# Two more sum banks for the last stage, later edge walks, last stores behind a load, and zero products in the pauses of a four-layer graph kernel

## The reference

```python
agg = segment_sum(h[src], dst) / max(deg, 1)      # SAGE, twice: relu(conv 1), then conv 2
out = agg @ W_l + b + h @ W_r
out = segment_sum((h @ W)[src] * edge_weight, dst) + b            # GCN
agg = segment_sum(concat(h[src], edge_attr) @ W_message, dst)     # message
z = layernorm(relu(agg) + h); z = z + mlp(z) (3 layers with skips); out = layernorm(h + z)
out = h @ W_self + segment_sum(top32(h @ W_neigh)[src], dst) / max(deg, 1)   # MaxK
```

## Time and profile before

| | |
|---|---|
| median of the runs | 1699.55 us |
| the profiled execution | 1700.06 us, span 1698.3 us |
| TensorE busy | 93% of the span |
| VectorE, ScalarE, GpSimd busy | 57%, 37%, 19% |
| DMA | 145 GB/s in the mean |

### The profile page before, as it was taken

The page is one execution under the profiler, slowest core; times in us unless marked ns, Lnnn a source line. Parts: engine busy times, 40 slices in busy tenths (PEclk is TensorE's granted clock), DMA queues, the critical chain, the costliest instruction groups (busy, mean ns, idle before and its releaser), DMA issues.

```text
span 1698.3 us, 41805 instructions
## 1 busy us (share of the span) xinstructions
PE 1580.5 (93%) x11011; PEld 1223.6 (72%) x11012; DVE 960.0 (57%) x2841; ACT 627.2 (37%) x1718; POOL 330.3 (19%) x926
## 2 busy tenths in 40 slices
PE   2899999999979999899997999999999999996996
PEld 1555565555657777678886888888878888874885
DVE  5788888878842122232335666666636777774111
ACT  6677787877731111111112222222224444440000
POOL 1565675656620000000000000000012111120000
PEclk8999999999999999999999999999999999997998
DMA  4266575757596766433354655666432221211444
GB/s 133 70 171 180 145 207 146 199 147 205 146 270 198 204 193 193 136 114 118 133 161 124 168 160 160 169 174 177 120 111 71 80 80 62 79 60 69 146 153 153
DMA packets 353541, 245.57 MB, mean 145 GB/s; under 512 B 195242, under 2 KB 337382, under 8 KB 353510
## 3 DMA queue, kind: packets, MB, share of 16 engines
q1 hardware_dynamic: 353510, 245.19, 50.4%
HBM read 138.17 MB, written 99.31 MB: 140 GB/s over the span
## 4 chain that ended last, share of the span: by engine, by line
issue 60%; PE 32%; DVE 3%; POOL 2%; DVEq 1%; SPq 0%; DMA 0%; POOLq 0%
PE ps L1386 21%; PE ps L1475 8%; POOL work L651 2%; PE ps L1429 1%; PE ps L1427 1%; DVE e_buf L1005 1%; DVE work L951 0%; PE ps L1421 0%; DMA arena<-turned_blocks 0%; SPq L419 0%; PE ps L1362 0%; DVE small L1262 0%; PE ps L1374 0%; DVE e_buf L1021 0%; PE ps L1379 0%
## 5 line engine op out<-in xcount | busy, mean ns | idle before, releaser
L1475 PE MATMUL ps<-arena 128*128 128x256 f16 (+1 forms) x5000 | 610.5, 274 | 21.8 <-DMA arena<-cnt_blocks 8.2
L1475 PEld LDWEIGHTS ps<-arena 128*128 128x128 f16 x5000 | 488.4, 98 | 122.9 <-issue 53.5
L1386 PE MATMUL ps<-e_buf 128*128 128x400 bf16 (+1 forms) x2476 | 376.6, 308 | 23.6 <-DVE e_buf L1005 23.5
L1386 PEld LDWEIGHTS ps<-e_buf 128*128 128x128 bf16 x2476 | 219.1, 98 | 169.9 <-DVE e_buf L1005 53.9
L1469 PE MATMUL ps<-arena 128*128 128x256 f32 x1250 | 278.5, 379 | 1.3 <-DMA arena<-wgt_blocks 1.3
L1469 PEld LDWEIGHTS ps<-arena 128*128 128x128 f32 x1250 | 235.4, 190 | 32.4 <-issue 1.5
L636 POOL TENSOR_SCALAR e_buf<-e_buf,w_col 128x128 bf16<-128x128 bf16 x600 | 225.0, 390 | 159.4 <-DVE e_buf L1001 152.1
L651 POOL TENSOR_TENSOR work<-work 128x256 f32<-128x256 f32 x75 | 54.5, 727 | 995.9 <-ACT work L844 995.9
L1005 DVE TENSOR_SCALAR e_buf<-iota,off_g,front 128x400 bf16<-128x400 f16 (+1 forms) x619 | 220.2, 402 | 32.9 <-issue 21.3
L1001 DVE TENSOR_SCALAR e_buf<-iota,front 128x128 bf16<-128x128 f16 x419 | 114.7, 279 | 44.4 <-PE ps L1386 30.0
L677 ACT ACTIVATE e_buf<-e_buf,front 128x128 bf16<-128x128 bf16 x219 | 88.3, 403 | 106.7 <-DVE e_buf L1001 104.9
(11 more groups left out here) (214 smaller groups left out, 1571.4 us busy)
## 6 DMA issues: line engine op xcount, KB each, us to landing
arena<-turned_blocks SPq DMA_DIRECT2D x75, 800.0 KB, 4.3
wgt_blocks<-arena SPq DMA_DIRECT2D x25, 1600.0 KB, 10.3
arena<-wgt_blocks SPq DMA_DIRECT2D x25, 1600.0 KB, 8.3
cnt_blocks<-work SPq DMA_DIRECT2D x25, 800.0 KB, 5.5
turned_blocks<-arena SPq DMA_DIRECT2D x25, 800.0 KB, 3.6
e_raw<-edge_features_padded SPq DMA_DIRECT2D x25, 576.0 KB, 7.8
edge_features_padded<-in_edge_attr SPq DMA_DIRECT2D x24, 512.0 KB, 9.9
out<-arena SPq DMA_DIRECT2D x24, 128.0 KB
```

Source lines behind the costliest of these rows:

```text
L1386: return pe.matmul(bank[:, 0:wide], rows_, cols, start=start, stop=True, skip_group_check=True)
L1475: m = pe.matmul(agg[par][:, 0:wide], BLK16[par][:, b * P:(b + 1) * P], ZH[zin(i)][:, b * ZW + part * D:b * ZW + part * D + wide], start=(b ...
```

## The change

Four things change. TensorE runs products of a zero tile with itself into bank 7 in four pauses of the preparation. The last chunk's counts are still stored ahead of load(2), but its weights behind it, and its edge features behind the third turn of late weights; ScalarE's wait for that weights store moves to the first z. In `row_layer`, walk 0 moves behind the first blocks of tile 1 and walk 1 behind tile 1, and `early` behind tile 1. In the last stage tiles 2 and 3 have sum banks 7 and 5 and blocks in the unused upper halves of the buffers, and are begun early too; the tiles from 4 on run as before. The diff, cut:

```diff
@@ sync
-            def store(c, par):
-                pad_edges(c)
+            def store_counts(c, par):
                 wait(sp, s_taken, c * PER + (PER + CR))
                 sp.dma_start(cnt_dram[...], ...).then_inc(s_store_c[par], 16)
+            def store_weights(c, par):
                 sp.dma_start(wgt_dram[...], ...).then_inc(s_store_w[par], 16)
...
-            store(NT - 1, 0)
+            store_counts(NT - 1, 0)
...
                     load(2, 2, 1, 0)
+                    store_weights(NT - 1, 0)
                     load(3, 3, 1, 1)
...
                     for turn in range(3):
                         keep_and_load(2 + turn, turn)
+                    pad_edges(NT - 1)
...
+                elif i == 4:
+                    for n in range(2):
+                        load(n, NT * i + n, None, n)
+                    for n in range(2):
+                        sp.dma_start(BLKX[n], turned_dram[2 + n]).then_inc(s_blkx[n], 16)
+                    tiles(sp, i, load, first=4)
@@ scalar, sage1
                     copy_transpose(g - 2, par)
+                    act.wait_ge(s_store_w[0], 16 * (NPAIR + 1))
                     first_z(n - 2, g - 2, par, ZH[1], conv_scale)
                 if isinstance(n, int) and n == 1:
                     act.wait_ge(s_scale, SCALE_CONV)
-                    for par_ in range(2):
-                        act.wait_ge(s_store_w[par_], 16 * ((NT + 1 - par_) // 2))
+                    act.wait_ge(s_store_w[1], 16 * NPAIR)
@@ vector, last
-                chain(dve.scalar_tensor_tensor(out=urow, in0=agg[1 - par][:, 0:D], scalar=one(rdeg, n),
+                from_ = agg_x[n - 2] if isinstance(n, int) and n in (2, 3) else agg[1 - par]
+                chain(dve.scalar_tensor_tensor(out=urow, in0=from_[:, 0:D], scalar=one(rdeg, n),
...
-            tiles(dve, PH_MAXK, last)
+            for n in range(4):
+                last(n, NT * PH_MAXK + n, None, (NT * PH_MAXK + n) % 2)
+            tiles(dve, PH_MAXK, last, first=4)
@@ tensor, preparation
+            def keep_running(rounds):
+                with pe.Fori(0, rounds):
+                    for k in range(8):
+                        pe.matmul(ps[:, 7, 0:P], zeros[:, :], zeros[:, :], start=True, stop=True,
+                                  skip_group_check=True)
             pe.wait_ge(s_const, 10)
+            keep_running(18)
             pe.wait_ge(s_prep, PREP_ROWS)
...
+            keep_running(14)
             pe.wait_ge(s_prep, PREP_SCAN)
...
+            keep_running(16)
             pe.wait_ge(s_prep, PREP_STEPS - 3)
...
+            keep_running(7)
             pe.wait_ge(s_prep, PREP_STEPS)
@@ tensor, aggregate
-            def aggregate(i, n, q, h, par, b0, b1):
-                if b0 == 0:
-                    wait(pe, s_blk[par], h * 16 + 16)
+            def aggregate(i, n, q, h, par, b0, b1, further=False):
+                into, counts = (agg_x[par], BLKX[par]) if further else (agg[par], BLK16[par])
+                if b0 == 0 and further:
+                    wait(pe, s_blkx[par], 16)
+                elif b0 == 0:
+                    wait(pe, s_blk[par], h * 16 + (0 if i == 4 and not (isinstance(n, int) and n < 2) else 16))
                     wait(pe, s_aggfree, q - 1 + CR)
@@ tensor, row_layer
-                if beside:
-                    beside(0)
                 z_ready(i)
                 aggregate(i, 0, q0, q0 // 2, q0 % 2, NT - 1, NT)
-                if early:
-                    early()
                 def body(n, q, h, par):
                     ...
                     aggregate(i, n, q, h, par, 0, c0)
                     if beside:
-                        beside(n)
+                        beside(0 if isinstance(n, int) and n == 1 else n)
                     transpose_rows(q + (NT - 1), par)
                     ...
-                tiles(pe, i, body, first=1, peel=1 if late_step else 0)
+                body(1, q0 + 1, (q0 + 1) // 2, (q0 + 1) % 2)
+                if early:
+                    early()
+                if beside:
+                    beside(1)
+                tiles(pe, i, body, first=2)
@@ tensor, inter and the last stage
-                    elif n < NT + 2 and b0 < final:
-                        begun_early(4, b0, min(b1, final), n - NT)
+                    elif n < NT + 4 and n != NT + 2 and b0 < final:
+                        begun_early(4, b0, min(b1, final), n - NT if n < NT + 2 else 2)
...
+            begun_early(4, final_early, NT - 2, 2)
+            begun_early(4, 0, NT - 2, 3)
             z_ready(4)
-            for n in range(2):
+            for n in range(4):
                 q = NT * 4 + n
-                aggregate(4, n, q, q // 2, q % 2, NT - 2, NT)
-            tiles(pe, 4, lambda n, q, h, par: aggregate(4, n, q, h, par, 0, NT), first=2)
+                aggregate(4, n, q, q // 2, q % 2, NT - 2, NT, further=(n >= 2))
+            tiles(pe, 4, lambda n, q, h, par: aggregate(4, n, q, h, par, 0, NT), first=4)
```

More of the change, by code:

```diff
@@ L97, in build @@
         assert 5 * PREP <= ZF + BLKF and 2 * BLKF <= ZF
+        BLKX = [region(o_blk + b * BLKF + BLKF // 2, BLKF // 2).bitcast(F16) for b in range(2)]
         spare = region(o_blk + BLKF + BLKF // 2, BLKF // 2)
@@ L173, in build @@
         agg = [ps[:, b, :] for b in range(2)]
+        agg_x = [ps[:, 7, :], ps[:, 5, :]]
         tp = [ps[:, 2 + b, 0:D] for b in range(2)]
@@ L219, in build @@
         s_blk = [sem(f"block_loaded{b}") for b in range(2)]
+        s_blkx = [sem(f"further_block_loaded{b}") for b in range(2)]
         s_agg = sem("aggregated")
@@ L469, in _ @@
                 for c in range(2):
-                    store(j * 2 + c, c)
+                    pad_edges(j * 2 + c)
+                    store_counts(j * 2 + c, c)
+                    store_weights(j * 2 + c, c)
             def load_turned(n, par):
@@ L1468, in aggregate @@
                     if i == 2:
-                        m = pe.matmul(agg[par][:, 0:D], BLK32[par][:, b * P:(b + 1) * P],
+                        m = pe.matmul(into[:, 0:D], BLK32[par][:, b * P:(b + 1) * P],
                                       ZFULL[0][:, b * D:(b + 1) * D], start=(b == 0), stop=(b == NT - 1),
@@ L1474, in aggregate @@
                     for part, wide in ((1, D + (i == 0)), (0, D)):
-                        m = pe.matmul(agg[par][:, 0:wide], BLK16[par][:, b * P:(b + 1) * P],
+                        m = pe.matmul(into[:, 0:wide], counts[:, b * P:(b + 1) * P],
                                       ZH[zin(i)][:, b * ZW + part * D:b * ZW + part * D + wide],
@@ L1490, in begun_early @@
                     pe.wait_ge(s, NT * i + b1 + CR)
-                aggregate(i, n, q, q // 2, q % 2, b0, b1)
+                aggregate(i, n, q, q // 2, q % 2, b0, b1, further=(i == 4 and n >= 2))
             def edge_walk(n):
@@ L1660, in top_multiply @@
                 m.then_inc(s_mm, 1)
+            final_early = 18
             def inter(n, h, par):
-                final = 18
+                final = final_early
                 if isinstance(n, int) and n > NT + 1:
```

## The result

The changed kernel takes 1686.8 us (median of 6 runs, 1682.8 to 1689.05), the kernel before beside it 1699.0 us: the ratio is 0.9925, with a 95% interval of 0.9913 to 0.9938, so it is faster by 0.6 to 0.9%. Four more runs of it in a later experiment gave 1683.5 us (1682.2 to 1690.2), ratio 0.9928 (0.9908 to 0.9948). The forecast was 1682.5, in a range of 1672 to 1692.

What follows compares the result with a forecast made beforehand. TensorE, busy for 93% of the span, was taken as the bound; its idle and low-clock time could go. -6.6 - 8.1 + 2.6 - 3.7 + 7.6 - 8.9 = -17.1 us gave 1682.5 us, range 1672 to 1692.

Steps and rivals of the forecast that it cites:

- Zero products: Preparation: zero products at 57 ns fill four pauses, so the work behind each runs at 2.4 GHz; -6.6 us.
- Building to SAGE1: Before tile 2 of SAGE1: load(2) goes out earlier, so the 6.46 us wait and its low clock go; -8.1 us.
- The wait before tile 3: Rival, SAGE1: the block wait moves from tile 2 to tile 3; +5 us, 1687.5 us; chance 0.11.
- The copies: SAGE1 before tile 10: edge-feature copies stand ahead of block 8's store in a queue without slack; +2.6 us.
- SAGE2: Start of SAGE2: tile 1 runs without waiting for the maxima, then TensorE waits 2.05 us for row 0; -3.7 us.
- GCN: Start of GCN: TensorE idles some 11 us for row 0 behind VectorE's next split; +7.6 us, between +4 and +11.
- Last stage: Step to the last stage: 92 products of tiles 2 and 3 run early, around 7.62 us of idle time; -8.9 us.
- Its 0.9 us: Last stage: 36 early products in the last step hold up the last row; +0.9 us on the path.
- the others: Among them: zero products at 83 ns, 1689 us, chance 0.12; late walks cost nothing, 1675 us, chance 0.11.
- Later tiles of GCN do not wait: Answers a rival: the GCN wait repeats in each tile, 5.4 us for a row, 1807 us; chance 0.02.
- zero operands release the clock: Answers a rival: zero products don't release the clock, run at 107 ns and overrun the pauses, 1704.5 us; chance 0.06.

Runs made afterwards that it cites:

- The two experiments on it: Against the changed kernel: later GCN walks undone, 1678.0 us; later walks kept, but row 0 handed out ahead of the second edges' split, 1676.8 us.

## Why the prediction was right, and where it was off

Each step, in us, from the profiles of the kernel before and of two executions of the changed kernel. The steps are cut at fixed instructions of TensorE: the first product of SAGE1 (483.96, 478.05 and 475.73 us), the last products begun early for SAGE2 (719.40, 711.12, 706.20), the transposes of SAGE2's last row (891.99, 880.55, 875.33), those of GCN's row 2 (945.86, 942.97, 936.29) and the end. So the first row holds the building too, whose length differs by up to 1.5 us between profiles, and the last one the rest of GCN and the message stage.

| step | forecast | first profile | second profile |
|---|---|---|---|
| preparation, to the first product of SAGE1 | -6.6 | -5.9 | -8.2 |
| building to SAGE1, and the copies | -5.5 | -2.4 | -5.0 |
| SAGE2 | -3.7 | -3.2 | -3.5 |
| GCN | +7.6 | +8.5 | +7.1 |
| last stage | -8.9 | -10.4 | -8.4 |
| sum (of unrounded values) | -17.1 | -13.3 | -18.0 |

- **Zero products.** Right in mechanism and size. My 57 ns was the line through wider products, and 112 products with a weight load each took 6.43 us. The Trainium skill's 81 ns ("TensorE: Matmul & The Clock Gate", Back-to-back issue gap) does not hold here, where they took 57. The first fill ran for 5.9 us (4.5 in the second profile) at 107 ns, for which I had taken 4, and ended at 16.1 us (15.6), just in time. What I had not priced: the clock can fall again between two fills; where it did, the third fill overran and about 1.5 us of the 6.6 were lost.
- **Building to SAGE1.** The wait before tile 2 went, as forecast, by load(2) going out at 483.89. From the transposes of the first tile's mean to the ninth's the stage is 6.0 us shorter in the first profile and 8.1 in the second, against -8.1. The wait before tile 3, a rival at +5, came at +1.28 in the first profile and not in the second.
- **The copies** are the term that was mis-sized: +2.6 forecast, +4.5 and +4.2 measured over the two tiles around the wait (22.6 and 22.3 us for 18.1). The added wait was forecast well (3.76 for "about 3.5"); I left out that the clock falls behind such a wait, as it did in both profiles: the 18 products behind it took 3.30 us, not 2.15, and those after them also ran slower.
- **SAGE2** as worked out: 2.05 us of waiting in place of 3.37, and 3.5 us gained; in the first profile 0.3 of it was lost again at the stage's end. No run undoes the moved maxima alone, so this gain is read from the traces.
- **GCN** as worked out: one wait of 11.50 us for "some 11", the clock low behind it, +7.1 to +8.5 for +7.6. Walk 2 and row 1 wait too, for 3.07 and 0.52 us (3.08 and 1.92 in the second profile), as the forecast's own times for row 1 imply; from row 2 on the tiles are unchanged. The two experiments on it show that VectorE's order is the reason.
- **Last stage.** -8.2 alone, -8.4 in the second profile: the term of -8.9 was right. Its 0.9 us came only where the clock fell behind the 2.39 us wait, which the forecast had not made a condition; the -10.4 of the first profile is an execution in which it did not fall there and was low for less time behind the block.
- **The rivals**: the wait at tile 3 came at a quarter of its price; of the others none took place. Later tiles of GCN do not wait, and zero operands release the clock.

So the median of the first six runs, 4.3 us above the forecast, is made of falls of the clock that come in some executions, of the copies' term and of the 1.28 us before tile 3; that the last stage came out 1.5 us better than forecast in the first profile hid a part of it. What stays open is what decides, in a single execution, whether the clock falls behind a wait of 1 to 3 us.

## What to carry to other kernels

When work on one engine is moved later, look at what stands behind its result on the engine that takes it: here the walk itself cost nothing, and VectorE's next split, which stood between it and the row that TensorE needed, made TensorE wait for 11.5 us. Where a queue has no slack, as at tile 10, an added transfer comes out as a wait, and the wait can be paid twice, once as idle time and once as low clock. Waits that can't be removed can be filled with products of zeros, as long as these end before the wait does; the pauses of the preparation and the 4 us of the last stage show it.

## What the runs showed of the hardware

- In one execution the clock fell behind an idle time of 1.15 us (window 28.30) and stayed up behind one of 2.39 us (window 1531.50); in the second execution of the same code it was the other way round (windows 10.00 and 1525.40). The Trainium skill ("TensorE: Matmul & The Clock Gate", What's actually happening) says that the chip's watching of TensorE is not aligned with the kernel, so that one kernel differs from run to run. The traces agree: at each of these places, and behind the 11.5 us wait in GCN, the two executions differ by about 1.5 us.
- Products of zeros by zeros took 107 ns each at the low clock and 56 to 63 ns at the high one. Where 64 of them filled the 4 us wait of the last stage, the clock stayed at 1.00 (window 1530.50); in the eleven profiles without them it fell.
- VectorE stood for 2.8 to 4.8 us at the first instruction behind its SAGE1 loop, in all thirteen profiles, with nothing in the profile that releases it.
